# Two-layer graph network on one core: one-hot row picking from slot 12 for fourteen groups, and layer-1 pieces moved behind slot 145

## What is computed

```python
edge_index = jnp.stack([src, dst])
x = _layernorm(x + _L0_gnn_ref(x, edge_weight, src, dst, Wm, bm, W1, b1, W2, b2))
x = _layernorm(x + _L1_gnn_ref(x, edge_index, W1l, b1l, W1r, W2l, b2l, W2r))
```

```python
msgs = z[edge_dst] @ Wd + z[edge_src] @ Ws + edge_weight[:, None] * ww[None, :] + bm
agg = jax.ops.segment_max(msgs, edge_dst, num_segments=n)   # 0 where a node has no edge
hidden = jax.nn.relu(z @ W1a + agg @ W1b + b1)
return hidden @ W2 + b2
```

## Time and profile before

| | us |
|---|---|
| median of three runs (1100.16 to 1101.87) | 1100.61 |
| the profiled execution, its own time | 1098.6 |
| its span, first to last instruction | 1096.8 |
| PE busy | 1020.9 (93%) |
| DVE busy | 852.8 (78%) |
| POOL busy | 739.7 (67%) |
| ACT busy | 671.0 (61%) |

### The profile page before, as it was taken

The page is one execution under the profiler, slowest core; times in us unless marked ns, Lnnn a source line. Parts: engine busy times, 40 slices in busy tenths (PEclk is TensorE's granted clock), DMA queues, the critical chain, the costliest instruction groups (busy, mean ns, idle before and its releaser), DMA issues.

```text
span 1096.8 us, 25699 instructions
## 1 busy us (share of the span) xinstructions
PE 1020.9 (93%) x7183; PEld 756.1 (69%) x7183; DVE 852.8 (78%) x2994; ACT 671.0 (61%) x1741; POOL 739.7 (67%) x782
## 2 busy tenths in 40 slices
PE   4898989999999999999999999998988989899997
PEld 4576667777777777776767777766666666657786
DVE  6598788888878878887979888987877877645465
ACT  3345778988887778877867887433233333313664
POOL 7767777777777777777777777777777777201332
PEclk9898999999999999999999999999999999999999
DMA  8654434344334434434444443543444353545321
GB/s 204 166 130 114 96 98 103 94 100 119 95 102 106 107 104 107 101 94 128 107 102 92 104 94 98 144 107 88 115 132 104 101 148 99 147 127 164 80 59 42
DMA packets 130203, 121.29 MB, mean 111 GB/s; under 512 B 24126, under 2 KB 115573, under 8 KB 130053
## 3 DMA queue, kind: packets, MB, share of 16 engines
q1 hardware_dynamic: 103624, 70.53, 24.5%
q0 software_dynamic: 23328, 47.82, 18.0%
q10 hardware_dynamic: 3101, 1.21, 0.5%
HBM read 105.60 MB, written 13.88 MB: 109 GB/s over the span
## 4 chain that ended last, share of the span: by engine, by line
PE 48%; POOL 27%; issue 13%; ACT 4%; DVE 3%; DMA 2%; ACTq 2%; DVEq 0%; SPq 0%
POOL area L1100 27%; PE bank L1833 9%; PE bank L1735 8%; PE bank L1959 7%; PE bank L1724 5%; PE bank L1802 4%; PE bank L1675 4%; PE bank L1714 3%; PE bank L1663 2%; PE bank L1924 2%; ACT area L949 1%; PE bank L1910 1%; DMA area<-zs_d,area 1%; ACT hot_r L957 1%; ACTq L889 1%
## 5 line engine op out<-in xcount | busy, mean ns | idle before, releaser
L1100 POOL DMA_INDIRECT area<-zs_d,area x701 | 679.7, 970 | 216.4 <-issue 210.9
L896 ACT CAST adj_w<-bank 128x325 f32 x391 | 176.6, 452 | 312.7 <-PE bank L1735 244.7
L1286 DVE TENSOR_TENSOR_SCAN area<-area,bank 128x512 f32<-128x512 bf16 x196 | 249.6, 1274 | 141.1 <-PE bank L1675 122.2
L1270 DVE TENSOR_SCALAR area<-area 128x325 bf16<-128x325 f16 x782 | 252.2, 323 | 0.0
L1735 PE MATMUL bank<-area 128*128 128x104 f32 x1564 | 225.1, 287 | 0.2
L1269 DVE TENSOR_SCALAR area<-area 128x128 bf16<-128x128 f16 x782 | 209.3, 268 | 5.4 <-PE bank L1735 5.3
L1735 PEld LDWEIGHTS bank<-area 128*128 128x128 f32 x1564 | 196.1, 197 | 10.6 <-issue 2.0
L1833 PE MATMUL bank<-hot_r,zs_r 128*128 128x512 f32 x600 | 176.1, 420 | 1.9 <-ACT hot_r L957 1.2
L1724 PE MATMUL bank<-area 128*128 128x325 bf16 x782 | 151.5, 307 | 9.8 <-DVE area L1271 5.4
L949 ACT ACTIVATE area<-adj_w,node_c 128x512 bf16<-128x512 f32 x225 | 156.5, 744 | 0.0
L1675 PE MATMUL bank<-ident,area 128*128 128x128 f32 x706 | 117.1, 289 | 27.5 <-DMA area<-zs_d,area 27.1
(11 more groups left out here) (175 smaller groups left out, 1105.9 us busy)
## 6 DMA issues: line engine op xcount, KB each, us to landing
area<-mask_d SPq DMA_DIRECT2D x195, 128.0 KB
area<-zs_d,area POOLq DMA_INDIRECT x701
area<-zs_d SPq DMA_DIRECT2D x640, 0.5 KB
area<-parts_d SPq DMA_DIRECT2D x20, 384.0 KB, 6.8
area<-wp_d SPq DMA_DIRECT2D x195, 9.0 KB
adj_w<-in_src_dram SPq DMA_DIRECT2D x12, 256.0 KB
zr_d<-area SPq DMA_DIRECT2D x24, 128.0 KB
area<-zr_d SPq DMA_DIRECT2D x6, 512.0 KB, 3.9
```

The costliest lines, as they stand in the source:

```text
L896: nc.scalar.copy(adj[:, :, bass.ds(at, W)], A_BANK[s % 2][:, 0:COLS].rearrange("p (h w) -> p h w", w=W))
L1100: pool.indirect_dma_start(gring[:, g % GR * 4 + s % 2 * 2 + u, :], None, x if g < RAW else zs_d[0:N, :], bass.IndirectOffsetOnAxis(ap=firs ...
L1270: nc.vector.tensor_scalar(hot_d[:, r, u, :], i_key[:, 0:COLS], key_n[:, u, s:s + 1], None, ALU.is_equal)
L1286: nc.vector.tensor_tensor_scan(S[:, g % 2, 0:n], mask[:, g % MR, 0:n], (G_BANK if g in PICKED else T_BANK[g % 2])[:, 0:n], S[:, (g + 1) % ...
```

## The change

`PICKS` is now made from a list of ends: fourteen groups are picked, not twelve, and picking begins in slot 12, not 19. The first two stretches have nine slots each, the others 8 to 11 (before: nine slots in the first four, then eleven). The splits of the table and its loads move forward (`SPLITS`, `SOURCE_SLOTS`). DVE makes no one-hot of the first two picked groups (u below 50), then every fourth as before; in all it makes 75, as before, and ACT 275, before 225. Of the layer-1 pieces the five that began in slots 102, 104, 113, 115 and 117 are gone from there. Behind slot 145 there are now twelve pieces of four tiles (before seven, in slots 145 to 161), each whole in one slot. The number of pieces and all their work stay the same.

```diff
-PICKS = ((28, 19), (37, 28), (46, 37), (55, 46), (66, 55), (77, 66), (88, 77), (99, 88), (110, 99), (121, 110), (132, 121), (143, 132))
+ENDS = (21, 30, 39, 47, 56, 67, 78, 88, 97, 106, 114, 123, 133, 144)
+PICKS = tuple(zip(ENDS, (12,) + ENDS))
 PICKED = tuple(g for g, _ in PICKS)
-SPLITS = ((11, 0, 8), (13, 8, 16), (15, 16, 24), (16, 24, NT))
-SOURCE_SLOTS = (8, 10, 12, 13)
+SPLITS = ((7, 0, 8), (8, 8, 16), (10, 16, 24), (11, 24, NT))
+SOURCE_SLOTS = (5, 6, 7, 8)
...
+    for q, js, at in ((0, (2, 3), (145, 146)), (1, (2, 3), (147, 148)), (2, range(4), (150, 151, 152, 153)), (3, range(4), (155, 156, 160, 161))):
+        for j, s in zip(js, at):
+            made.append((s, j, 4 * q, 4 * q + 4, j == js[0]))
...
+def in_one_slot(s, j):
+    return j == 5 or 145 <= s <= 161
...
 def by_vector(u):
-    return u % 4 == 3
+    return u >= 2 * NT and u % 4 == 3
```

More of the change, by code:

```diff
@@ L91, in plan @@
     made = []
[L92 to L102, removed]
+    for s, q, js in ((49, 0, (0,)), (70, 0, (1,)), (81, 1, (0, 1))):
+        for n, j in enumerate(js):
+            made.append((s + 2 * n, j, 4 * q, 4 * q + 4, n == 0))
+    for q, js, at in ((0, (2, 3), (145, 146)), (1, (2, 3), (147, 148)), (2, range(4), (150, 151, 152, 153)), (3, range(4), (155, 156, 160, 161))):
+        for j, s in zip(js, at):
+            made.append((s, j, 4 * q, 4 * q + 4, j == js[0]))
     for j in range(4):
@@ L1363, in usual @@
                     for c, s, j, h0, h1, _ in pieces(k, 1) + pieces(k):
-                        if (s if j == 5 else s + (h1 - h0) // 2 - 1) == k:
+                        if (s if in_one_slot(s, j) else s + (h1 - h0) // 2 - 1) == k:
                             add_piece(c, j, j not in [p[1] for p in PIECES[:c]])
@@ L1857, in usual @@
                             raw_T(g)
-                    for c, _, j, h0, h1, _ in pieces(k, 1):
-                        if h1 - h0 == 4 and j < 5:
+                    for c, s, j, h0, h1, _ in pieces(k, 1):
+                        if h1 - h0 == 4 and not in_one_slot(s, j):
                             half_piece(c, j, h0, h1, h0 + 2)
-                    for c, _, j, h0, h1, _ in pieces(k):
+                    for c, s, j, h0, h1, _ in pieces(k):
                         half_piece(c, j, h0, h1, h0)
-                        if h1 - h0 == 4 and j == 5:
+                        if h1 - h0 == 4 and in_one_slot(s, j):
                             half_piece(c, j, h0, h1, h0 + 2)
```

## The result

The changed kernel takes 1117.2 us (median of six, 1110.75 to 1118.69), the kernel before, run beside it, 1100.78: a ratio of 1.0138, 95% interval 1.0115 to 1.0162. It is 16.4 us slower, where 3.7 were forecast. The direction was right; the size is outside the range. The profiled execution took 1116.72 for a span of 1114.9.

The account below looks back on a forecast made before the run. POOL's gathers bound the kernel; POOL issues group g only after PE's transposes of slot g-4 (the ring). POOL's 10.1 us gain less 13.8 of waits for PE gave +3.7: 1098.6 + 3.7, plus 2.0 for the median, 1104.3; range 1100 to 1109.

Parts of the forecast that it names:

- POOL sets the end; behind it nothing changes: POOL's last gather ends the slots at 939.3; the 157.5 us after it are not touched by the change.
- POOL gains 10.1: Two more picked groups save eight gathers of 1.26 us, -10.1 us, if POOL waits nowhere.
- PE's shift at slot 31, +8.0: ACT's serial work from slot 12, 90.6 us, makes slot 31 begin on PE at 181.8, not 173.82; bounds +3 and +10.
- the 86.3 that I keep: Slot 12's start on ACT in the kernel before, 86.34, kept as the start of ACT's serial sum.
- PE from slot 31 to 131, -1.6: More one-hots +13.7, picked slots -0.5, pieces gone -13.1, row waits -2.7, register-load waits +1; PE +6.4 at slot 131.
- +1 (bounds 0 and +3): Slots 31 to 131: added PE idle, mostly behind ACT's register loads, with an eighth more one-hots on ACT.
- From 131 to 156, +7.2: Late pieces +10.5, row waits gone -4, bank waits +0.7; PE +13.6 at slot 156, less 9.9 gives +3.7.
- the two slacks: PE's room before POOL must wait: 3.7 us from slot 131 to group 135, 9.9 from slot 156 to group 160.
- The third rival: PE waits for a whole DVE scan in each of seven neighbouring late pieces: +12.6, 1113.2 us; chance 0.08.
- the fourth: DVE sets the pace; its one-hots and scans stay, so the time stays 1100.6 us; chance 0.04.
- The first two rivals: By slot 31 ACT does not hold PE (+0, 1096.3 us, chance 0.19) or holds it half as long (+4, 1100.3, 0.21).
- What would show it: Signs: POOL's waits for PE 14 to 19 us, behind group 31 to before 160; slot 31 near 182, last gather near 943.

Follow-up runs that it names:

- l: Changed kernel with the edits of a and h, slot 83's layer-1 piece moved behind slot 145 and four late pieces behind slot 166; 1089.4 us, ratio 0.9917.
- a: Changed kernel with VectorE again making every fourth one-hot of the first two picked groups; 1105.5 us, ratio 1.0048.
- g: Kernel before with ScalarE making all one-hots of the first two picked groups (slots 19 to 36); 1107.2 us, ratio 1.0070.
- c: Kernel before with only the change's early source loads and table splits; 1100.5 us, ratio 1.0005.
- h: Changed kernel with ScalarE loading eight registers every fourth slot, not sixteen every eighth; 1103.9 us, ratio 1.0039.
- d: Kernel before with only the five layer-1 pieces moved behind slot 145, one slot each there; 1097.5 us, ratio 0.9978.
- b: Changed kernel with the five layer-1 pieces back in slots 102 to 118 and every piece in two slots; 1121.6 us, ratio 1.0216.
- j: Changed kernel with the edits of both a and h; 1094.2 us, ratio 0.9949.
- k: Kernel before with ScalarE loading eight registers every fourth slot, not sixteen every eighth; 1097.1 us, ratio 0.9977.

## Why the prediction failed, step by step

- *POOL sets the end; behind it nothing changes.* Right: 157.6 us to 157.5.
- *POOL gains 10.1.* Right as a floor: kernel l has 8.6 of it.
- *PE's shift at slot 31, +8.0.* The mechanism, ScalarE's serial work, is right (a, g); the term was mis-sized: +14.2. ScalarE's stretch from slot 12 to the first copy of slot 29 took 183.05 - 90.47 = 92.6 for the 90.6 summed, and it began at 90.47 and not at 86.34. The failing sentence is that the moved splits and loads "cost nothing at the end" and are "in the 86.3 that I keep". They made VectorE's one-hots late in slot 12, PE waited 0.82 and 1.81, ScalarE waited 1.90 for PE (c shows the same start, 90.59, with these lines alone). A delay at the door of an engine that is full behind it is paid in full: 4.1 of the missing 6.2. The prediction also set 2 us too little for the stretch itself, of which 1.2 are further waits for PE.
- *PE from slot 31 to 131, -1.6.* It came out at +6.3. PE's idle time grew by 1.4 (7.7 to 9.1) where it was to shrink by 1.7. The rows' waits went as forecast; the mis-sized term is the "+1 (bounds 0 and +3)" for PE's waits behind register loads: the waits for ScalarE's copies alone grew by 3.4, from 3.6 to 7.0 (waits for one-hots by another 0.7). PE's busy time grew by 4.8 (454.3 to 459.1) where one-hots, picked slots and pieces were summed to +0.1. One term was missing there: the fall of the granted clock behind such waits, 3.4. Without it, in h, PE was busy 455.7, so the sum of one-hots and pieces was 1.3 too low.
- *From 131 to 156, +7.2.* It came out at +5.6. This place was taken for the deciding one, by 1.0. Whatever the shift ahead of both, slot 156 decides only if this term is above 6.2, the difference of the two slacks; it was not, so slot 131 did (16.7 to 16.1). A part of the rest is the clock of the kernel before, 0.98 in this stretch where the changed kernel had 1.00: some 2 us of 109, an estimate, which the prediction left out. The third rival, late pieces that wait for VectorE, has no support in d, b or the rows above; the fourth, VectorE's pace, none either.
- *The first two rivals* needed ScalarE to hold PE by at most half of what was forecast; it held it longer.
- *What would show it.* ScalarE next to no idle time from 86 to 177: right from 90.5 on, but for its register loads and the 1.2 us named above. PE's idle time under 10 from slot 31 to 131: right (9.1). Slot 31 near 182, waits of 14 to 19: 188 and 41.1. First wait behind group 31: wrong, the first new one above 0.3 us is at group 22, at 119.4. Last one before group 160: right for waits above 0.4, it is at group 135.

The change as a whole, then: two picked groups were worth nearly what they were taken for (8.6 of 10.1 in l), and the pieces moved well. The one line that handed twelve one-hots to ScalarE cost 10 to 12 us, and fourteen groups on ScalarE's long register loads 11 to 13.

## What to carry to other kernels

Where a ring couples two engines, take the deciding shift as the latest, over all places, of the follower's shift less the slack there, and list every place with little slack: two were not enough (in g slot 118 decided, in h and j a place ahead of slot 131). An engine that is about to be filled without gaps pays for each delay at its entrance, so work out when it really starts, not when it started before. A cost that lies in slack now (k: 2.4 us) can be worth over 10 once the pace-setter changes; put a bound on it by all the waits that can stand behind it, not by a part of one row.

## What the runs showed of the hardware

- A load of sixteen registers held ScalarE mostly 2.58 to 2.65 us, one of eight mostly 0.91 to 0.94 (four times 1.20 to 1.32): two short ones cost less than one long.
- In the changed kernel between slots 31 and 131, with PE next to fully busy, waits of 0.8 and 1.3 us in a picked slot were each followed by some 3 us at the lower clock; a wait of 1.10 ahead of 244.50, in a slot that is not picked, was not. In kernel a one of 1.07 in a slot that is not picked, ahead of 232.06, was. What decides it stays open.
- Six executions of the changed kernel spread over 7.9 us (the fastest, 1110.75, has the highest mean clock, 0.986), six of the kernel before, beside it, over 1.7, but 23 of it on another chip over 5.8. That the clock makes the spread is not shown.
